# Four-layer graph network on one core: the preparation ahead of the block walk in another order, with GpSimd taking over two of its parts

## What is computed

```python
edge_index = jnp.stack([src, dst])
h = relu(layernorm(x)); x = x + sage_two_layers(h, edge_index, ...)      # mean over neighbours, twice
h = relu(layernorm(x)); x = x + gcn(h, edge_weight, W, b, src, dst)      # weighted sum over neighbours
h = relu(layernorm(x)); x = x + interaction(h, edge_attr_64, src, dst)   # messages, MLP of three layers, two norms
h = relu(layernorm(x)); x = x + maxk(h, W_self, W_neigh, src, dst)       # top 32 of each row, mean over neighbours
```

## Time and profile before

| | us |
|---|---|
| median of 3 runs | 1649.49 (1647.69 to 1650.51) |
| profiled execution, its own time | 1648.47 |
| its span, first to last instruction | 1645.9 |
| granted TensorE clock, mean | 0.997 of full |

### The profile page before, as it was taken

One profiled execution on the slowest core, in us unless ns is written; L12 is line 12 of the kernel. 1 busy time (PEld: TensorE's weight loads), 2 busy tenths in 40 slices (PEclk: granted clock), 3 DMA queues, 4 the chain that ended last, 5 costly groups with the idle time before them and its releaser, 6 DMA issues.

```text
span 1645.9 us, 42637 instructions
## 1 busy us (share of the span) xinstructions
PE 1571.8 (95%) x11401; PEld 1231.4 (75%) x11402; DVE 967.3 (59%) x2866; ACT 620.7 (38%) x1693; POOL 327.5 (20%) x927
## 2 busy tenths in 40 slices
PE   7899998999999999999999999999999999998996
PEld 7555555555567777778888888888888888886885
DVE  6888897888861222243335666666646777777111
ACT  6777787777741111111112222222224444441000
POOL 1565565665530000000000000000002222220000
PEclk9999999999999999999999999999999999999998
DMA  4366585766698776533345666666632222131344
GB/s 138 91 183 161 154 208 145 186 177 161 170 243 229 224 206 188 173 115 124 119 156 148 165 165 165 165 166 168 172 110 71 76 83 83 62 137 65 120 142 154
DMA packets 353545, 245.62 MB, mean 149 GB/s; under 512 B 195242, under 2 KB 337382, under 8 KB 353510
## 3 DMA queue, kind: packets, MB, share of 16 engines
q1 hardware_dynamic: 353510, 245.19, 52.3%
HBM read 138.17 MB, written 99.31 MB: 144 GB/s over the span
## 4 chain that ended last, share of the span: by engine, by line
issue 60%; PE 32%; DVE 3%; POOL 3%; DVEq 1%; SPq 0%; POOLq 0%; DMA 0%; ACT 0%
PE ps L1429 22%; PE ps L1522 8%; POOL work L675 3%; PE ps L1471 1%; DVE e_buf L1021 1%; PE ps L1464 0%; DVE work L967 0%; DVE e_buf L1017 0%; SPq L424 0%; PE ps L1708 0%; DVE e_buf L1037 0%; DVEq L396 0%; DVEq L1017 0%; DVEq L1021 0%; PE ps L1402 0%
## 5 line engine op out<-in xcount | busy, mean ns | idle before, releaser
L1522 PE MATMUL ps<-arena 128*128 128x256 f16 (+1 forms) x5000 | 602.4, 272 | 6.6 <-DVEq L320 1.6
L1522 PEld LDWEIGHTS ps<-arena 128*128 128x128 f16 x5000 | 484.7, 97 | 101.3 <-issue 32.6
L1429 PE MATMUL ps<-e_buf 128*128 128x400 bf16 (+1 forms) x2476 | 381.2, 307 | 30.1 <-DVE e_buf L1021 20.3
L1429 PEld LDWEIGHTS ps<-e_buf 128*128 128x128 bf16 x2476 | 213.0, 97 | 190.7 <-DVE e_buf L1021 64.7
L1516 PE MATMUL ps<-arena 128*128 128x256 f32 x1250 | 278.7, 380 | 2.4 <-DMA arena<-wgt_blocks 2.4
L1516 PEld LDWEIGHTS ps<-arena 128*128 128x128 f32 x1250 | 235.8, 190 | 33.7 <-issue 1.7
L675 POOL TENSOR_TENSOR work<-work 128x256 f32<-128x256 f32 x75 | 59.8, 797 | 957.9 <-ACT work L860 957.9
L1021 DVE TENSOR_SCALAR e_buf<-iota,off_g,front 128x400 bf16<-128x400 f16 (+1 forms) x619 | 231.0, 416 | 32.6 <-PE ps L1429 20.5
L660 POOL TENSOR_SCALAR e_buf<-e_buf,w_col 128x128 bf16<-128x128 bf16 x600 | 216.6, 375 | 165.8 <-DVE e_buf L1017 165.4
L701 ACT ACTIVATE e_buf<-e_buf,front 128x128 bf16<-128x128 bf16 x219 | 88.0, 402 | 108.4 <-DVE e_buf L1017 108.2
L1017 DVE TENSOR_SCALAR e_buf<-iota,front 128x128 bf16<-128x128 f16 x419 | 102.0, 251 | 35.5 <-PE ps L1429 23.4
(11 more groups left out here) (215 smaller groups left out, 1585.7 us busy)
## 6 DMA issues: line engine op xcount, KB each, us to landing
arena<-turned_blocks SPq DMA_DIRECT2D x75, 800.0 KB, 4.3
wgt_blocks<-arena SPq DMA_DIRECT2D x25, 1600.0 KB, 10.3
arena<-wgt_blocks SPq DMA_DIRECT2D x25, 1600.0 KB, 8.7
cnt_blocks<-work SPq DMA_DIRECT2D x25, 800.0 KB, 5.5
turned_blocks<-arena SPq DMA_DIRECT2D x25, 800.0 KB, 3.8
e_raw<-edge_features_padded SPq DMA_DIRECT2D x25, 576.0 KB, 3.9
edge_features_padded<-in_edge_attr SPq DMA_DIRECT2D x24, 512.0 KB, 9.9
out<-arena SPq DMA_DIRECT2D x24, 128.0 KB
```

The lines of the kernel that those rows point to most:

```text
L1429: return pe.matmul(bank[:, 0:wide], rows_, cols, start=start, stop=True, skip_group_check=True)
L1522: m = pe.matmul(into[:, 0:wide], counts[:, b * P:(b + 1) * P], ZH[zin(i)][:, b * ZW + part * D:b * ZW + part * D + wide], start=(b == 0 an ...
```

## The change

The order of the preparation is changed on DVE and PE, and POOL gets two jobs.

- DVE computes the destination group first, and at once its extremes (two reductions), then copies one turned array (the weights, which PE transposes as soon as the edges are loaded) from PSUM, then does the rest of the number work. Its eight operations of the weight split are gone.
- PE turns the extremes with the statistic's column broadcast to 128 columns, so that each row of extremes stands on all 128 partitions. DVE copies and scans them there (`scan` has 128 partitions now). The product that spread the scanned rows (L1415) is gone, and the eight counts read the scanned rows from SBUF instead of PSUM.
- The other three turned arrays are copied after the 17 table operations, while PE turns the table.
- POOL sums the last ten node tiles (15 to 24) by folding: 256 columns to 128, 64, 32 and so on to 1, eight additions over ten tiles, a drain between them. It begins when `s_x[3]` and `s_x[4]` are in. ACT sums the first 15, and waits for both (`s_mean` at 2).
- POOL then splits the weights: six copies and two subtractions of 512 elements, a drain after each. DVE and ACT wait for it (`s_weights`) ahead of the walk.
- ACT runs one activation of one column ahead of the sums. PE's rounds of zeros are 4, 4, 11 and 6.

```diff
-PREP_ROWS = 6 + 2 + 5 + 2
-PREP_SCAN = PREP_ROWS + 4 + 8 + 4
-PREP_STEPS = PREP_SCAN + 8 * 1 + 17 + 3
+PREP_STAT = 4
+PREP_ROWS = PREP_STAT + 1 + 4 + 7
+PREP_TABS = PREP_ROWS + 4 + 8 + 17
+PREP_STEPS = PREP_TABS + 3 + 3
...
+ON_ACT = 3 * SB
...
-        scan = work[0:1, 4:8, :].rearrange("o (a b) d -> o a (b d)", a=2)
+        scan = work[:, 4:8, :].rearrange("p (a b) d -> p a (b d)", a=2)
...
+            pool.wait_ge(s_x[3], 16)
+            pool.wait_ge(s_x[4], 32)
+            folded = R_[:, ON_ACT:NT, :]
+            chain(pool.tensor_tensor(folded[:, :, 0:P], X[:, ON_ACT:NT, 0:P], X[:, ON_ACT:NT, P:D], ALU.add))
+            wide = P // 2
+            while wide > 1:
+                chain(pool.tensor_tensor(folded[:, :, 0:wide], folded[:, :, 0:wide], folded[:, :, wide:2 * wide], ALU.add))
+                wide //= 2
+            pool.tensor_tensor(row_sum[:, ON_ACT:NT].rearrange("p (n o) -> p n o", o=1), folded[:, :, 0:1],
+                               folded[:, :, 1:2], ALU.add).then_inc(s_mean, 1)
+            pool.wait_ge(s_prep, PREP_STAT + 1)
+            w16 = ring[:, 0:NCOL]
+            for k in (C_W0, C_W1):
+                chain(pool.tensor_copy(w16, col[:, k, :]))
+                chain(pool.tensor_tensor(col[:, k + 1, :], col[:, k, :], w16, ALU.subtract))
+                chain(pool.tensor_copy(col[:, k, :], w16))
+            chain(pool.tensor_copy(w16, col[:, C_W2, :]))
+            chain(pool.tensor_copy(col[:, C_W2, :], w16))
+            pool.sem_inc(s_weights, 1)
             pool.wait_ge(s_rs, 1)
...
             act.wait_ge(s_const, 10)
-            for j in range(NT // SB):
-                act.wait_ge(s_x[j], 16 * (1 + (j == NT // SB - 1)))
+            act.activation(small[:, 15:16], eps_outer, ACT.Copy)
+            for j in range(ON_ACT // SB):
+                act.wait_ge(s_x[j], 16)
...
-            act.wait_ge(s_mean, 1)
+            act.wait_ge(s_mean, 2)
...
             act.wait_ge(s_prep, PREP_STEPS)
+            act.wait_ge(s_weights, 1)
...
-            dve.tensor_scalar(pi[2], Dd, 3, None, ALU.arith_shift_right).then_inc(s_prep, 1)
+            chain(dve.tensor_scalar(pi[2], Dd, 3, None, ALU.arith_shift_right))
+            chain(dve.tensor_copy(pf[4], pi[2]))
+            for a, op in enumerate((ALU.max, ALU.min)):
+                dve.tensor_reduce(stat[:, a, :], part_f[:, 4], AX.X, op).then_inc(s_prep, 1)
...
+            dve.wait_ge(s_prep_pe, EB)
+            dve.tensor_copy(col[:, C_W0, 1:NCOL], ps[:, C_W0, 0:NCOL - 1]).then_inc(s_prep, 1)
...
-            for a in range(4):
-                dve.wait_ge(s_prep_pe, EB * (a + 1))
-                dve.tensor_copy(col[:, a, 1:NCOL], ps[:, a, 0:NCOL - 1]).then_inc(s_prep, 1)
...
-            chain(dve.tensor_copy(w16, col[:, C_W0, :]))
-            chain(dve.tensor_tensor(col[:, C_W1, :], col[:, C_W0, :], w16, ALU.subtract))
...
+            big, low = scan[:, 0, 0:ET], scan[:, 1, 0:ET]
+            high_of_tile, low_of_tile = ps[:, 4, 0:ET], ps[:, 5, 0:ET]
+            dve.wait_ge(s_prep_pe, PE_STAT)
...
-            dve.wait_ge(s_prep_pe, PE_TABLES + 1)
...
-                chain(dve.tensor_scalar(count_scratch, ps[:, row, 0:ET], nidx[:, n:n + 1], 0.0, op, ALU.add,
+                chain(dve.tensor_scalar(count_scratch, scan[:, row, 0:ET], nidx[:, n:n + 1], 0.0, op, ALU.add,
...
+            for a in range(3):
+                dve.wait_ge(s_prep_pe, PE_STAT + EB * (a + 1))
+                dve.tensor_copy(col[:, a, 1:NCOL], ps[:, a, 0:NCOL - 1]).then_inc(s_prep, 1)
...
+            dve.wait_ge(s_weights, 1)
             dve.wait_ge(s_std, 1)
             dve.reciprocal(rs_all, sd_all).then_inc(s_rs, 1)
...
-            keep_running(18)
-            pe.wait_ge(s_prep, PREP_ROWS)
+            keep_running(4)
+            pe.wait_ge(s_rows, 16 * 3 * (EB + 1))
+            pe.wait_ge(s_pad, 3)
...
+            transpose_rows_of(C_W0, rows[:, 2])
+            pe.wait_ge(s_prep, PREP_STAT)
             for a in range(2):
                 for c in range(EB):
-                    m = pe.matmul(ps[0:1, 4 + a, c * P:(c + 1) * P], stat[:, a, c:c + 1], ident[:, :],
+                    m = pe.matmul(ps[:, 4 + a, c * P:(c + 1) * P], stat[:, a, c:c + 1].broadcast_to([P, P]), ident[:, :],
...
-            keep_running(14)
-            pe.wait_ge(s_prep, PREP_SCAN)
-            for k in range(2):
-                m = pe.matmul(ps[:, k, 0:ET], ones_row[0:1, :], scan[0:1, k, 0:ET], start=True, stop=True)
...
-            keep_running(16)
-            pe.wait_ge(s_prep, PREP_STEPS - 3)
+            keep_running(4)
+            pe.wait_ge(s_prep, PREP_ROWS)
+            for a, from_ in enumerate((part_f[:, 1], part_f[:, 8], part_f[:, 7])):
+                transpose_rows_of(a, from_)
+            keep_running(11)
+            pe.wait_ge(s_prep, PREP_TABS)
...
-            keep_running(7)
+            keep_running(6)
```

More of the change, by code:

```diff
@@ L48 @@
 LOWEST = -3.4e38
-PREP_ROWS = 6 + 2 + 5 + 2
-PREP_SCAN = PREP_ROWS + 4 + 8 + 4
-PREP_STEPS = PREP_SCAN + 8 * 1 + 17 + 3
+PREP_STAT = 4
+PREP_ROWS = PREP_STAT + 1 + 4 + 7
+PREP_TABS = PREP_ROWS + 4 + 8 + 17
+PREP_STEPS = PREP_TABS + 3 + 3
 ROUND = 1.5 * 2.0 ** 23
-PE_TABLES = 4 * EB + 2
+PE_STAT = EB + 2
+PE_TABLES = PE_STAT + 3 * EB
+ON_ACT = 3 * SB
 def build(nc, x, src, dst, edge_attr, edge_weight, w, out):
@@ L220, in build @@
         s_mean = sem("row_means_ready")
+        s_weights = sem("weights_split")
         s_rs = sem("row_factors_ready")
@@ L643, in _ @@
             pool.wait_ge(s_prep, PREP_STEPS)
-            pool.wait_ge(s_prep_pe, PE_TABLES + 2)
+            pool.wait_ge(s_prep_pe, PE_TABLES + 1)
             def second(n):
@@ L746, in _ @@
             m.then_inc(s_mean, 1)
-            act.wait_ge(s_mean, 1)
+            act.wait_ge(s_mean, 2)
             act.activation(nmean_all, row_sum, ACT.Copy, scale=-1.0 / D).then_inc(s_mean, 1)
-            act.wait_ge(s_mean, 2)
+            act.wait_ge(s_mean, 3)
             for n in range(NT):
@@ L914, in _ @@
             pf = [part_f[:, a].rearrange(whole) for a in range(9)]
-            dve.tensor_scalar(pi[2], Dd, 3, None, ALU.arith_shift_right).then_inc(s_prep, 1)
+            chain(dve.tensor_scalar(pi[2], Dd, 3, None, ALU.arith_shift_right))
+            chain(dve.tensor_copy(pf[4], pi[2]))
+            for a, op in enumerate((ALU.max, ALU.min)):
+                dve.tensor_reduce(stat[:, a, :], part_f[:, 4], AX.X, op).then_inc(s_prep, 1)
+            chain.v += 2
+            assert chain.v == PREP_STAT
+            dve.wait_ge(s_prep_pe, EB)
+            dve.tensor_copy(col[:, C_W0, 1:NCOL], ps[:, C_W0, 0:NCOL - 1]).then_inc(s_prep, 1)
             dve.tensor_scalar(pi[1], Dd, H - 1, None, ALU.bitwise_and).then_inc(s_prep, 1)
@@ L919, in _ @@
             dve.tensor_scalar(pf[6], S, 1.0 / HW, 0.5 / HW - 0.5, ALU.mult, ALU.add).then_inc(s_prep, 1)
[L920 to L924, removed]
+            chain.v += 4
+            dve.wait_ge(s_prep, chain.v)
+            chain(dve.tensor_copy(pf[3], pi[1]))
             chain(dve.tensor_scalar(pf[6], pf[6], ROUND, None, ALU.add))
@@ L933, in _ @@
             chain(dve.tensor_tensor(pf[8], pf[8], pf[6], ALU.add))
-            for a, op in enumerate((ALU.max, ALU.min)):
-                dve.tensor_reduce(stat[:, a, :], part_f[:, 4], AX.X, op).then_inc(s_prep, 1)
-            assert chain.v + 2 == PREP_ROWS, (chain.v, PREP_ROWS)
-            for a in range(4):
-                dve.wait_ge(s_prep_pe, EB * (a + 1))
-                dve.tensor_copy(col[:, a, 1:NCOL], ps[:, a, 0:NCOL - 1]).then_inc(s_prep, 1)
[L942 to L946, removed]
-            chain(dve.tensor_copy(w16, col[:, C_W0, :]))
-            chain(dve.tensor_tensor(col[:, C_W1, :], col[:, C_W0, :], w16, ALU.subtract))
[L949 to L959, removed]
+            assert chain.v == PREP_ROWS, (chain.v, PREP_ROWS)
+            big, low = scan[:, 0, 0:ET], scan[:, 1, 0:ET]
+            high_of_tile, low_of_tile = ps[:, 4, 0:ET], ps[:, 5, 0:ET]
+            dve.wait_ge(s_prep_pe, PE_STAT)
+            chain(dve.tensor_copy(big, high_of_tile))
+            chain(dve.tensor_copy(low, low_of_tile))
             chain(dve.tensor_tensor_scan(big, big, big, -1.0, ALU.max, ALU.max))
             chain(dve.tensor_tensor_scan(low[:, ::-1], low[:, ::-1], low[:, ::-1], 1e6, ALU.min, ALU.min))
-            assert chain.v == PREP_SCAN
-            dve.wait_ge(s_prep_pe, PE_TABLES + 1)
             def tiles_under(into, row, n, op):
-                chain(dve.tensor_scalar(count_scratch, ps[:, row, 0:ET], nidx[:, n:n + 1], 0.0, op, ALU.add,
+                chain(dve.tensor_scalar(count_scratch, scan[:, row, 0:ET], nidx[:, n:n + 1], 0.0, op, ALU.add,
                                         accum_out=into))
@@ L1000, in _ @@
                                            op1=ALU.add))
-            dve.wait_ge(s_prep_pe, PE_TABLES + 2)
+            assert chain.v == PREP_TABS, (chain.v, PREP_TABS)
+            for a in range(3):
```

(10 more changed lines are left out.)

7 lines of the change are left out of this document (2 added, 5 removed).

## The result

The changed kernel takes 1656.99 us in the median of 5 runs (1655.91 to 1661.25), the kernel before 1649.49 (1647.50 to 1650.98): ratio 1.0055, interval 1.0043 to 1.0067, thus 7.5 us more. The profiled execution took 1655.91 us, its span 1654.2 against 1645.9 before: 8.3 us more. The time around the span, which I took as fixed at 2.6 us, is 1.7 us here, so by the times of these two executions it is 7.4 us. Busy time of PE fell by 9 us (1562.9), as there are fewer zeros; that is no gain.

The account below looks back on a forecast made before the run. POOL's fold was taken to hold ACT, whose root holds DVE's reciprocal, with PE's clock low at first. Reciprocal +3.9, clock +2.1, PE's readiness -0.4 sum to +5.6 us: 1655.1 us, range 1650.5 to 1659.5.

Parts of the forecast that it names:

- POOL's fold: POOL's eight additions and seven drains over ten tiles, after the last x lands: 8.3 us, ending at 30.1.
- ACT: ACT's sums wait for POOL's fold, start 6.3 us later, the rest unchanged; its root ends at 44.5.
- Reciprocal: DVE's reciprocal ahead of the walk waits for ACT's root and comes at 44.6 instead of 40.65, 3.9 us later.
- DVE ready at 31.9: DVE's preparation up to its last casts, in the new order, is done at 31.9 instead of 40.65, 8.7 us early.
- Rival A: POOL's additions collide with DVE's counts and table operations; fold 2.4 us longer, +8.0, 1657.5 us; chance 0.12.
- The split: POOL's weight split after the fold takes 6.8 to 12.6 us, hidden behind ACT's 14.3 us of squares.
- PE's clock: After about 13 us of rest PE begins the walk at half rate: loses 2.1 us, with 0.4 credited for earlier readiness.
- The sum: Whole kernel: +3.9 + 2.1 - 0.4 = +5.6 us, giving 1655.1 us.
- The walk and the layers behind it shift as they are: After the preparation, the walk and the layers keep their lengths and only move by the sum, +5.6 us.
- Rival B: No measurable change: DVE's gain meets POOL's cost, with full clock and PE's readiness worth 1.1; 1649.1 to 1651.9 us; chance 0.18.
- C: Faster: ACT's path not held by POOL; a 3.3 us gain wants a fold of 1.1 us or less; chance 0.05.
- D: POOL's split, not ACT's root, ends last, needing over 14.3 us for eight operations; +7.6, 1657 us; chance 0.03.

Follow-up runs that it names:

- more zeros: Against the kernel with early squares, late split and copies: PE's zeros lengthened to 24 and 12 rounds from 11 and 6; 1646.15 us, ratio 0.9977.
- early squares with the late split and copies: Changed kernel without fold; ACT squares 15 tiles early, root activation first; POOL's split after DVE's scans; eight idle DVE copies added: 1645.05 us, ratio 0.9962.

## Why the prediction was right in its sum and wrong in one step

The mechanism was the one forecast: POOL's fold holds ACT, ACT holds the reciprocal, and PE begins the walk at the low clock. The time, 1656.99 us, is 1.9 above the forecast of 1655.1 and inside its range. That +5.6 and +5.45 lie so close at the walk's start is in part luck, since the reciprocal came 0.45 us earlier than forecast and the clock cost 0.3 more.

- **POOL's fold** (forecast 8.3 us, bounds 5.1 and 9.3, of which the lower adds up to 5.0): 21.80 to 29.66, 7.86 us. The line through two additions gave the first as 2.93 (measured 2.89); by the same line the seven drains cost 0.14 each and not 0.2.
- **ACT** (root to end at 44.5): 43.98. **Reciprocal** (+3.9): +3.45, released by ACT as forecast. Taking the fold out moved it by 6.0 us: shown.
- **DVE ready at 31.9**: wrong, 36.4. Until the last count it was right (25.33 against 25.3). The table operations took 6.4 us instead of 3.3, and PE turned the table in 2.72 us instead of about 1.5, with the granted clock at 0.57 from 28 to 36 us after 8.48 us of rest. Rival A had the meeting right and the side wrong: I charged POOL, which had its forecast price, and it was DVE that stood. The Trainium skill, "SBUF — State Buffer", "Who interferes with whom", was the better guide: the counts, which accumulate, stayed at 0.62 us beside POOL's additions, and where an operation with two SBUF inputs met an addition, it stood until that one had ended. In the kernels without the fold and with the fold alone, casts and operations with one SBUF input stood as well (1.39 and 3.10 us). DVE's loss changed nothing here, with 7.74 us of cover; in the kernel with the fold alone it decided the reciprocal.
- **The split** (6.8 to 12.6 us, hidden): 6.96, hidden. In the kernels without the fold its place decided where DVE was.
- **PE's clock** (lose 2.1, credit 0.4, net +1.7): lost 3.05, credit 1.05, net +2.0. Both terms were too small, and their errors cancel for the most part. The 2.1 came from the half rate of the zeros up to 10 us, 4.7 us long, but the row of 9 to 10 us has a granted clock of 1.00, so these rows didn't show the clock; here it was at 0.50 from the first product at 46.20 to about 52.
- **The sum** (+5.6): +5.45 at the second group, by which all its terms have come in.
- **"The walk and the layers behind it shift as they are"**: this step failed. The walk gave 0.75 us back (4.7 at its end), and the first layer took 2.8 more, by the pause and the wait for counts. I took DVE's eight missing instructions for a gain in time only and never asked what their places in the program were worth.
- Rival B had the credit for PE's readiness right (1.1), but its small case would have needed the full clock too, and C a fold of 1.1 us. Neither came. D: the split ended 7.4 us ahead of the root.

What stays open: profiles differ among themselves by 1 to 2 us in the waits for the counts' transfers and in later layers, so single steps behind 480 us are known no better, and with more zeros 1.4 us of an earlier walk did not show in the time. The best kernel by its median, early squares with the late split and copies, is 6.3 us faster than the kernel before; that its zeros or copies are at their best isn't shown.

## What to carry to other kernels

Before freeing the engine that ends a stage last, look up who ends second: here ACT was done only 2.45 us ahead of DVE, and work put on a slower engine behind the last data to land made ACT's chain 6 us longer. Give GpSimd its work beside Vector operations that accumulate or that copy out of PSUM, not beside ones that read and write SBUF (here casts, one-input and two-input arithmetic all stood), and look for the loss on both engines. When a loop far behind an edit becomes slower once, with "issue" as the only reason, count the instructions in front of it, and pad them as a test before believing in another cause.

## What the runs showed that was not expected

- A Vector operation of two elements took 1.03 us instead of 0.16, and a cast of 512 elements 3.10 instead of 0.43, while a GpSimd addition ran.
- Eight instructions fewer in DVE's program brought a pause of 2.5 to 4.0 us in the first layer, of which PE lost 0.9 to 2.3.
- After a root, copies and squares ran on ACT with no further table load, and the later root needed none: 1.28 us off its path.
- The granted clock was 0.51 from 48.0 to 51.3 us though PE had run zeros up to 44.2 and was at work on the walk's sparse first products from 46.0.
